# Turning the probabilities of a masked attention layer with two half-size DMA transposes in place of one

## The reference, cut to what matters

```python
q = heads(x @ Wq + bq); k = heads(x @ Wk + bk); v = heads(x @ Wv + bv)
scores = einsum('bhqd,bhkd->bhqk', q, k) * scale
scores = where(mask[:, None] == 0, -inf, scores)
attn = softmax(scores, axis=-1)
out = einsum('bhqk,bhkd->bhqd', attn, v)
out = out.transpose(0, 2, 1, 3).reshape(b, s, D_MODEL)
x = layernorm(x + out @ Wo + bo)
```

## Time and profile before

| | |
|---|---|
| median of 3 runs | 970.38 us (966.47 to 970.94) |
| the profiled execution's own time | 969.65 us |
| its span, first to last instruction | 967.9 us |
| mean granted TensorE clock | 0.975 |
| TensorE busy | 884.4 us (91%) |
| VectorE busy | 824.4 us (85%) |
| ACT busy | 686.0 us (71%) |
| POOL busy | 274.1 us (28%) |
| DMA packets' time, share of 16 engines | 66.6% |

### The profile page before, as it was taken

How to read it: one execution, slowest core, us unless ns; L and a number is a source line. 1 busy time by engine, 2 the same in 40 slices (tenths; PEclk the granted TensorE clock), 3 DMA queues, 4 the chain that set the end, 5 groups by cost and what they waited for, 6 DMA issues and landing times.

```text
span 967.9 us, 34884 instructions
## 1 busy us (share of the span) xinstructions
PE 884.4 (91%) x11784; PEld 606.3 (63%) x11784; DVE 824.4 (85%) x3449; ACT 686.0 (71%) x1745; POOL 274.1 (28%) x386
## 2 busy tenths in 40 slices
PE   6899989999999999999999999999999999999654
PEld 4666556666666666666666666666666666666321
DVE  5778888998999898889998889989999989998851
ACT  5766777777777777777777777777777777777640
POOL 0212233332323333232333323233232323322211
PEclk9999999999999999999999999999999999999876
DMA  7376777776667777666676766677676667667551
GB/s 283 62 135 127 138 151 160 166 159 146 145 141 157 161 164 160 147 145 141 155 166 158 167 146 141 144 156 162 157 168 147 147 140 157 157 157 148 94 119 50
DMA packets 362287, 143.33 MB, mean 148 GB/s; under 512 B 340752, under 2 KB 344848, under 8 KB 361872
## 3 DMA queue, kind: packets, MB, share of 16 engines
q1 hardware_dynamic: 362256, 142.93, 66.6%
HBM read 42.21 MB, written 16.78 MB: 61 GB/s over the span
## 4 chain that ended last, share of the span: by engine, by line
PE 36%; DVE 28%; DMA 19%; issue 10%; SPq 5%; DVEq 1%; ACT 0%; POOL 0%; POOLq 0%
PE proj_ps L610 29%; DMA aT<-a_pair 13%; DVE masked L496 9%; DVE p_pair L483 8%; DMA pT<-p_pair 6%; SPq L253 5%; PE score_ps L610 4%; PE av_ps L610 4%; DVE stats L525 2%; DVE y L522 2%; DVE qT_lo L476 2%; DVE a_pair L462 1%; DVE kT_lo L476 1%; DVE minus_max L496 1%; DVE inv_sum L505 1%
## 5 line engine op out<-in xcount | busy, mean ns | idle before, releaser
L410 ACT ACTIVATE probs<-masked,minus_max 128x128 f32<-128x128 f32 x1024 | 326.8, 390 | 215.1 <-DVE minus_max L496 212.6
L496 DVE CUSTOM_DVE_ANT_0 masked<-score_ps,mask 128x128 f32<-128x128 f32 x1024 | 236.2, 286 | 83.5 <-PE score_ps L610 75.2
L610 PE MATMUL proj_ps<-wo_hi,aT 128*128 128x512 f16 x512 | 169.1, 392 | 30.3 <-DMA aT<-a_pair 27.3
L483 DVE SCALAR_TENSOR_TENSOR p_pair<-probs,p_pair 128x512 f16<-128x512 f32 x256 | 195.0, 762 | 1.1 <-ACT p_pair L420 1.0
L420 ACT ACTIVATE p_pair<-probs 128x512 f16<-128x512 f32 x256 | 161.3, 630 | 24.9 <-DMA pT<-p_pair 10.5
L610 PEld LDWEIGHTS av_ps<-v_parts,pT 128*128 128x128 f16 x3072 | 111.2, 96 | 76.3 <-DMA pT<-p_pair 25.4
L610 PE MATMUL proj_ps<-xT_hi,wq_hi 128*128 128x256 f16 x512 | 141.6, 276 | 10.9 <-DVE wq_lo L579 8.3
L610 PE MATMUL av_ps<-v_parts,pT 128*128 128x33 f16 (+1 forms) x3072 | 117.1, 177 | 33.6 <-DMA pT<-p_pair 31.2
L225 POOL TENSOR_TENSOR xT_lo<-xT_raw,xT_hi 128x512 f16<-128x512 f32 x60 | 73.6, 1227 | 246.2 <-ACT xT_hi L373 246.2
L610 PE MATMUL proj_ps<-xT_hi,wk_hi 128*128 128x256 f16 x512 | 140.2, 274 | 1.2 <-DVE qT_lo L476 1.0
L610 PE MATMUL proj_ps<-xT_lo,wq_hi 128*128 128x256 f16 x512 | 141.0, 275 | 0.0
(11 more groups left out here) (58 smaller groups left out, 1538.9 us busy)
## 6 DMA issues: line engine op xcount, KB each, us to landing
xT_raw<-x_cols SPq DMA_DIRECT2D x32, 512.0 KB, 4.0
x_in<-x_rows SPq DMA_DIRECT2D x32, 512.0 KB, 3.7
out<-y SPq DMA_DIRECT2D x64, 256.0 KB, 2.2
adj_in<-adj SPq DMA_DIRECT2D x32, 128.0 KB, 2.3
pT<-p_pair SPq DMA_TRANSPOSE x256, 3.1
w_land<-weights SPq DMA_DIRECT2D x2, 1024.0 KB, 7.9
w_land<-weights SPq DMA_DIRECT2D x4, 256.0 KB, 6.1
x_res<-weights SPq DMA_DIRECT2D x1, 1024.0 KB, 10.0
```

The source lines that it names most:

```text
L410: ins = act.activation(probs[s % 2][:, j * S:(j + 1) * S], masked[s % 2][:, j], ACT.Exp, bias=minus_max[s % 2][:, j:j + 1], scale=-1.0)
L483: dve.scalar_tensor_tensor(out=p_pair[s % 2][:, HW:2 * HW], in0=probs[s % 2][:], scalar=P_UP, in1=p_pair[s % 2][:, 0:HW], op0=ALU.mult, op ...
L496: ins = dve.tensor_tensor_reduce(masked[s % 2][:, j], score_ps[j][:, s % HC], mask[par][:, s // KC], -EXP_SCALE, 3.0e38, ALU.add, ALU.min, ...
L610: return pe.matmul(dst, lhsT, rhs, start=first, stop=last)
```

## The change

SP now turns the high part of a slot's probabilities (columns 0 to 511 of `p_pair`, four blocks) as soon as ACT has written it, and the low part (columns 512 to 1023) in a second DMA as soon as VectorE has written that. The wait for a free pT buffer (`av_done`) stands ahead of the high half. The two halves together add 32 to `p_turned`, and the two waits on it ask for 32 for each round. The transposes of `a_pair` stay whole; in the new file they stand at line 265, those of the probabilities at 253 (high) and 256 (low).

```diff
             def turn_probs(g, s):
                 u = unit(g, s)
+                sp.wait_ge(p_hi_done, u + 1)
+                sp.sem_inc(sync_goes, 1)
+
+                wait(sp, av_done, u - NT + 1)
+                sp.sem_inc(sync_goes, 1)
+                sp.dma_start_transpose(pT[s % NT][:, 0:HC], p_pair[s % 2][:, 0:HW]).then_inc(p_turned[s % NT], 16)
                 sp.wait_ge(p_lo_done, u + 1)
                 sp.sem_inc(sync_goes, 1)
-
-                wait(sp, av_done, u - NT + 1)
-                sp.sem_inc(sync_goes, 1)
-                sp.dma_start_transpose(pT[s % NT][:], p_pair[s % 2][:]).then_inc(p_turned[s % NT], 16)
+                sp.dma_start_transpose(pT[s % NT][:, HC:2 * HC], p_pair[s % 2][:, HW:2 * HW]).then_inc(p_turned[s % NT], 16)
...
-                    act.wait_ge(p_turned[slot % NT], 16 * turn_round(before, slot))
+                    act.wait_ge(p_turned[slot % NT], 32 * turn_round(before, slot))
...
-                pe.wait_ge(p_turned[s % NT], 16 * turn_round(g, s))
+                pe.wait_ge(p_turned[s % NT], 32 * turn_round(g, s))
```

More of the change, by code:

```diff
@@ L247, in turn_probs @@
                 u = unit(g, s)
-                sp.wait_ge(p_lo_done, u + 1)
+                sp.wait_ge(p_hi_done, u + 1)
                 sp.sem_inc(sync_goes, 1)
@@ L252, in turn_probs @@
                 sp.sem_inc(sync_goes, 1)
-                sp.dma_start_transpose(pT[s % NT][:], p_pair[s % 2][:]).then_inc(p_turned[s % NT], 16)
+                sp.dma_start_transpose(pT[s % NT][:, 0:HC], p_pair[s % 2][:, 0:HW]).then_inc(p_turned[s % NT], 16)
+                sp.wait_ge(p_lo_done, u + 1)
+                sp.sem_inc(sync_goes, 1)
+                sp.dma_start_transpose(pT[s % NT][:, HC:2 * HC], p_pair[s % 2][:, HW:2 * HW]).then_inc(p_turned[s % NT], 16)
             def turn_attn(g, b):
```

## The result

| | before | with the change |
|---|---|---|
| median | 969.13 us (966.47 to 970.94, 4 runs) | 990.17 us (987.95 to 991.19, 4 runs) |
| profiled execution, its span | 969.65, 967.9 us | 990.2, 988.4 us |
| mean granted TensorE clock | 0.975 | 0.976 |

The ratio is 1.0216, 95% interval 1.0184 to 1.0248: the change makes the kernel slower by 21 us. The forecast was 949 us. The first rival, "the price is the instruction's", had said 987; how much of that nearness is luck stands under "Why the prediction was wrong".

A forecast was written before the change was run, and what follows sets the result against it. TensorE, busy 91% of the span, was taken to set the pace, with a transpose's 1.23 us issue on the critical path. Savings of 18.2 + 2.1 + 0.9 = 21.2 us off 969.65 gave 948.4, forecast 949 us, range 942 to 970.

The forecast's parts named there:

- The first rival: SP's queue: a half transpose costs the whole's 1.23 us, so SP becomes the late one; 987 us, chance 0.12.
- X: SP's queue: time one half-size transpose holds it, taken as 0.79 us, between 0.62 and 1.23.
- d: SP's queue: issue time saved ahead of aT, 1.23 - X = 0.44 us, range 0 to 0.61.
- the queue stays free, so this costs nothing: SP's queue: 256 more issues make 17.2 us of a 28.05 us group, so no loss.
- (a): Output projections: aT issued d earlier saves TensorE 0.44 and 0.20 us a group, 18.2 us in all.
- waited out for aT: Repeated groups: pT landing earlier gains nothing by itself, since TensorE then waits for aT at the first output projection.
- (b): pT's landing: 2.04 us after the low part, 1.06 sooner; worth 2.1 us at the start, 0.9 in the last group.
- (c): SP's queue: 256 added issues raise a group's issuing from 14.4 to 17.2 us, at no cost.
- left out of the sum: Waits inside a slot: two steps move off the low part's path, some tens of ns, not counted.
- (d): SP's new wait for the high part delays nothing behind it; ACT's wait to overwrite the buffer ends no later.
- VectorE: Second half of a group: VectorE can't follow the earlier TensorE, half the gain is lost; 959 us, chance 0.08.
- The rule to coalesce: DMA issue: coalesce small transfers; its section's formula gives 0.3 us a landing, none on the queue, 970 us.

The follow-up runs named there:

- run 1: Changed kernel with the transpose split into two and six blocks instead of four and four: 997.42 us, a single execution.
- run 4: Kernel before with aT's transpose issued ahead of the probabilities' one in slots 2 and 5: 963.07 us against 967.73, ratio 0.9952.
- run 7: Kernel before with the change's waits, in its order, ahead of one whole transpose: 962.68 us against 967.11, ratio 0.9954.
- run 10: Kernel before with the probabilities' transpose split in slot 2 alone: 981.12 us against 968.25, ratio 1.0132.
- run 8: Kernel before with aT issued first in slots 2 and 5, the change's moved waits, and loads moved to other slots: 948.61 us against 967.11, ratio 0.981.
- run 14: Kernel before with aT issued first in slots 2 and 5 and loads moved to other slots, without the moved waits: 950.69 us against 967.02, ratio 0.9823.
- run 2: Changed kernel with both halves issued only after the low part is written: 1082.36 us, a single execution.

## Why the prediction was wrong

**The step that failed is X**, the time for which half a transpose holds SP. I took 0.79 us by giving a transpose the fixed part of a plain transfer, 0.35, and letting the rest go by blocks; it measured 1.194. The rest was not the blocks': they cost 0.010 us each (run 1 and the change), and the fixed part is 1.15, three times that of a plain transfer. The argument "far above every plain one, so its blocks must carry most of it" compared two kinds of instruction, and said nothing about size. d is 0.04, not 0.44. With X fell the other half of the forecast, "the queue stays free, so this costs nothing": SP's 277.4 us of waiting went down to 0.6, and the queue became what sets the period.

**(a) aT earlier.** With d = 0.04 there was nothing to win. That pT's issue stands in front of aT, and that TensorE waits there for it, is shown by run 4, where the wait for aT vanishes. But the sum valued it too high, whatever X: run 4 takes all 1.23 us off and gains 4.7 us, not 22, since pT's wait takes over. I had said that the pT wait was "waited out for aT"; with aT out of the way it is the next bound, and the forecast needed a step for that.

**(b) pT earlier.** X + 0.69 + 0.56 was the right form: with X = 1.19 it is 2.44 us, measured 2.4. That it meets the half is in part luck. Its 1.37 us of data were read from a stretch in which the mask's load was issued too; and for two blocks the same form gives 1.17 + 0.34 + 0.56 = 2.07 us, where run 1 has 2.3.

**(c) What is added.** 17.2 us a group of issues was 23.6: 16 x 1.194 + 2 x 1.23 + 2.0. With gaps, 28.89 measured. The rival had the mechanism, and its 987 against 990.17 is better than its sum: with X = 1.194, which is at its own threshold of 1.19, it would have given 28.2 us a group, 3 us more in time over 28.5 groups. Its X of 1.23 was 0.04 too long, its gaps of 4.55 us 0.7 too short (5.24), and its 28.05 us for a group before was one group's; the average is 28.26. The errors nearly cancel, which is luck. The rival got the chance of 0.12 that my X left it. The tens of ns in the moved waits, "left out of the sum", were worth 4.4 us (run 7).

**(d)** was wrong in two points: where the queue is late, the high half stands in front of a low part that is already there. This alone costs 13 us in slot 2 (run 10). And ACT's wait for a free `p_pair` did not stay: 5.2 us before, 27.3 with the change.

**VectorE.** It never became the bound in the change. In run 8, 18 us faster, TensorE waits for its q parts more often than for anything else (27 times, 7.8 us), as that rival had placed it.

**The rule to coalesce** of the Trainium skill ("DMA: Bandwidth & Descriptors", "Rules for kernel authors") pointed the right way, and stood beside the rival that came nearest. The estimate from the Trainium skill's formula, which is for a DMA issued by GpSimd (no run here has one), was a landing 0.3 us sooner; the trace has 0.7. The formula has no term for the queue, which decided.

## What to carry to other kernels

Splitting a DMA to start its first part early can pay only while the queue that issues it stands waiting. Here it cost 13 us in one slot where the queue was late and 1.5 us in two where it was waiting, and no run shows a gain that is the split's alone. Look at that queue's own waits and at its timeline slot by slot, count every issue at its full price (here 1.1 to 1.3 us a transpose, whatever its size), and add up the period. If only one size of an instruction is in the trace, how its price goes with size is unknown, and both ends of the range deserve real weight. To bring one result forward, first see whether its issue can change places with one that isn't urgent: that, with the loads moved out of the way, gave 16 us here without adding an instruction (run 14).

## What was not expected of the hardware

- A DMA transpose holds SP for 1.172, 1.194, 1.215 and 1.232 us at two, four, six and eight blocks of 128 x 128 in float16, and 1.125 for one block of another tile, 0.04 below the line of the others. Where a half followed the other without a wait between (run 2), the second held it for 1.260. A plain transfer of 128 to 512 KB holds it for 0.35 to 0.45.
- Its landing does go with size: 2.2 us for the one block, 2.3, 2.4, 2.8 and 3.1 for two to eight.
- Four plain transfers a group issued by ACT instead of SP cost the unsplit kernel 57 us; aT's landing grew from 3.1 to 4.1 us and TensorE's wait for pT from 11.1 to 40.9. What delays them stays open.
- VectorE's low part took 1.58 us instead of 0.69 at some places (slot 2, at 507.23). The kernel before has such ones too (median 0.686, longest 1.676); why stays open. Over all slots the mean rose from 762 to 789 ns.
